# The first sort of a graph kernel carries each edge's weight beside its key, and the record gathers go

## The reference, cut to what matters

```python
x = _layernorm(x + segment_sum(x[src], dst))                        # L0: sum over incoming edges
# L1, ten times, with edge_src = dst and edge_dst = src:
up = jnp.maximum(f[edge_dst] - f[edge_src], 0.0) * sqrt(weights)[:, None]
f  = f + segment_max(up, edge_src)
# L2: three gated graph convolutions; each needs  nw[:, None] * (x @ W)[src]  summed by dst, nw from the edge weights
# L3: a four-layer MLP on (x_i, x_j - x_i) of every edge, averaged by dst
```

## Time and profile before

| what | us |
|---|---|
| three runs | 8461.82, 8480.76, 8480.96 |
| span of the profiled execution | 9642.0 |
| preparation, histogram 0, sort 0, until the first gather | 0 to 589 |
| rest of the sort stage | 589 to 1376 |
| L0 stage, main loop | 1376 to 2549 |
| busy: PE, DVE, ACT, POOL | 6289.8, 6437.2, 3431.3, 3063.5 |
| granted TensorE clock, mean | 0.880 |

### The profile page before, as it was taken

One profiled execution on the slowest core, in us unless ns is written; L12 is line 12 of the kernel. 1 busy time (PEld: TensorE's weight loads), 2 busy tenths in 40 slices (PEclk: granted clock), 3 DMA queues, 4 the chain that ended last, 5 costly groups with the idle time before them and its releaser, 6 DMA issues. The chain is left out here.

```text
span 9642.0 us, 139065 instructions
## 1 busy us (share of the span) xinstructions
PE 6289.8 (65%) x41922; PEld 3109.5 (32%) x41922; DVE 6437.2 (67%) x10345; ACT 3431.3 (36%) x4321; POOL 3063.5 (32%) x2943
## 2 busy tenths in 40 slices
PE   3100120028787979888898879788798989365555
PEld 2100120013443434334343434343344545222222
DVE  8864560017687878787787878787888989433333
ACT  0000000002255545555555555455444444132333
POOL 0047527740032323332232323332300000555553
PEclk9999985559899989999999989899899999677777
DMA  2000001128666667666676666566576767111110
GB/s 83 3 13 1 5 22 25 17 76 294 218 229 202 227 196 238 204 215 218 204 241 200 226 205 235 198 213 213 185 273 232 291 231 290 32 22 22 22 22 24
DMA packets 480504, 1461.81 MB, mean 152 GB/s; under 512 B 109553, under 2 KB 145049, under 8 KB 412582
## 3 DMA queue, kind: packets, MB, share of 16 engines
q1 hardware_dynamic: 228800, 1119.91, 33.6%
q10 hardware_dynamic: 157440, 298.89, 8.7%
q0 software_dynamic: 93568, 33.84, 3.0%
HBM read 1160.35 MB, written 292.22 MB: 151 GB/s over the span
## 5 line engine op out<-in xcount | busy, mean ns | idle before, releaser
L1435 PE MATMUL acc<-dst_hot,parts 128*128 128x512 bf16 x11600 | 3024.8, 387 | 575.1 <-issue 355.7
L1494 ACT ACTIVATE parts_out<-acc 96x1024 bf16<-96x1024 f32 x2320 | 2343.1, 1020 | 2018.0 <-PE acc L1446 1751.2
L1398 POOL DMA_INDIRECT group_best<-best_dram,best_row x1250 | 1361.0, 1089 | 3012.0 <-SPq L1361 2615.7
L1310 DVE TENSOR_SCALAR dst_hot<-dst_rows,node_f 128x2048 bf16<-128x2048 int16 x2910 | 2051.8, 740 | 180.1 <-PE acc L1446 138.7
L1435 PEld LDWEIGHTS acc<-dst_hot,parts 128*128 x11600 | 1057.6, 98 | 1868.2 <-issue 768.6
L914 POOL DMA_INDIRECT gathered<-table_dram,source_index x719 | 731.7, 1018 | 1800.2 <-POOLq L158 1300.5
L309 POOL DMA_INDIRECT got<-edges_dram,record_index x928 | 940.6, 1014 | 860.7 <-DVEq L777 548.8
L1446 PE MATMUL acc<-source,parts 128*128 128x128 bf16 x9280 | 922.6, 223 | 9.8 <-DMA source<-source_dram 4.5
L1446 PEld LDWEIGHTS acc<-source,parts 128*128 x9280 | 640.7, 99 | 642.7 <-issue 361.8
L1517 DVE SCALAR_TENSOR_TENSOR risen<-rise,factor 128x512 f32<-128x512 f32 x580 | 401.1, 692 | 588.0 <-PE rise L1458 322.3
L1523 DVE TENSOR_TENSOR_SCAN best<-joined,best,risen 128x512 f32<-128x512 uint8 x570 | 728.6, 1278 | 0.7
(11 more groups left out here) (376 smaller groups left out, 8013.5 us busy)
## 6 DMA issues: line engine op xcount, KB each, us to landing
dst_rows<-step_dst_dram SPq DMA_DIRECT2D x291, 1024.0 KB, 4.2
source<-source_dram SPq DMA_DIRECT2D x291, 1024.0 KB, 6.7
dst_kept_in<-dst_hot_dram SPq DMA_DIRECT2D x174, 1280.0 KB, 5.6
best_dram<-best_out ACTq DMA_DIRECT2D x580, 256.0 KB
factor<-step_weight_dram ACTq DMA_DIRECT2D x560, 256.0 KB
sources<-source_dram SPq DMA_DIRECT2D x174, 512.0 KB, 6.6
dst_hot_dram<-dst_kept SPq DMA_DIRECT2D x58, 1280.0 KB
src_rows<-step_src_dram SPq DMA_DIRECT2D x58, 512.0 KB
```

The costliest lines, as they stand in the source:

```text
L1310: nc.vector.tensor_scalar(hot[k % 2][b][:, :], index_rows[k // 2 % 2][:, k % 2, :], node_f[:, b:b + 1], None, ALU.is_equal).then_inc(hot_r ...
L1398: pool.indirect_dma_start(group_best[:, g, h, :], None, best_dram, bass.IndirectOffsetOnAxis(ap=best_row[:, i:i + 1], axis=0)).then_inc(en ...
L1435: nc.tensor.matmul(acc[n % 3][:, 0:TILE], blocks[b], hot[k % 2][b][:, q * TILE:(q + 1) * TILE], start=(b == 0), stop=(b == DST_BLOCKS - 1))
L1494: act.activation(moved[n % (2 * QUADS)][:, :], acc[n % 3][0:SPLIT, :], ACT.Copy).then_inc(tile_moved, 1)
```

## The change

The low 17 bits of key 0 now hold the destination's number within its group, plus one (`dst_id`), in place of the edge number. `record`, `edges_dram`, `got`, `record_index`, `group_base` and all 928 gathers go. The weights are loaded into `load[0]`, and each of the 153 stages of sort 0 has three instructions more on VectorE: a comparison of the keys into a mask in PSUM (`out_of_order`), and two predicated copies that exchange the weights (`swap_loads`, called at the head of the next stage, or in `turn` and at the end). Before them ScalarE has copied the whole weight array (`keep_loads`, 128 x 1024). At each turn TensorE transposes the weights as well, and ScalarE copies them. After the sort the weights are stored, loaded back as rows, and turned as the keys are; destinations, weights and roots for L0 and L1 come from these in `slots_by_group`, and are stored in the sort stage. Sort 1 is as before.

```diff
-            for n in range(k * STEP_SUBS, (k + 1) * STEP_SUBS):
-                pool.indirect_dma_start(got[:, n, :], None, edges_dram,
-                                        bass.IndirectOffsetOnAxis(ap=record_index[:, n:n + 1], axis=0)).then_inc(got_in, 16)
...
+                    link(nc.vector.scalar_tensor_tensor(dst_id[0:EP, :], group_key, -float(DST_NODES), dst_in[0:EP, :], ALU.mult, ALU.add))
+                    link(nc.vector.tensor_scalar(dst_id[0:EP, :], dst_id[0:EP, :], 1, None, ALU.add))
...
+            def sort_tensor(pe, turn_ready, turned_done, copied, swapped=None, load_turned=None, load_moved=None):
                 for n in range(turns):
                     pe.wait_ge(turn_ready, n + 1)
                     if n:
                         pe.wait_ge(copied, n)
+                    turn_blocks(turned, ping[0]).then_inc(turned_done, 1)
+                    if swapped:
+                        pe.wait_ge(swapped, STAGES_BEFORE[n])
+                        if n:
+                            pe.wait_ge(load_moved, n)
+                        turn_blocks(load_t, load[STAGES_BEFORE[n] % 2]).then_inc(load_turned, 1)
...
+            def keep_loads(act, s, swapped, kept):
+                if s:
+                    act.wait_ge(swapped, s)
+                act.activation(load[(s + 1) % 2][:, :], load[s % 2][:, :], ACT.Copy).then_inc(kept, 1)
...
+            def sort_scalar_loaded(act, turned_done, copied, loaded, swapped, kept, load_turned, load_moved):
+                act.wait_ge(loaded, 1)
+                for s in range(len(STAGE_BITS)):
+                    if s in STAGES_BEFORE:
+                        n = STAGES_BEFORE.index(s)
+                        act.wait_ge(turned_done, n + 1)
+                        act.activation(ping[0][:, :], turned[:, :], ACT.Copy).then_inc(copied, 1)
+                        act.wait_ge(load_turned, n + 1)
+                        act.activation(load[s % 2][:, :], load_t[:, :], ACT.Copy).then_inc(load_moved, 1)
+                        act.wait_ge(load_moved, n + 1)
+                    keep_loads(act, s, swapped, kept)
...
+                def swap_loads():
+                    s = done[1]
+                    if not swapped or s == done[0]:
+                        return
+                    m = STAGE_BITS[s]
+                    was, to = halves(load[s % 2], m), halves(load[(s + 1) % 2], m)
+                    greater = out_of_order[s % 2].rearrange("p (n w) -> p n w", w=1 << m)
+                    dve.wait_ge(kept, s + 1)
+                    nc.vector.copy_predicated(to[0], greater, was[1])
+                    nc.vector.copy_predicated(to[1], greater, was[0]).then_inc(swapped, 1)
+                    done[1] += 1
 
                 def stage(m):
+                    swap_loads()
+                    a, z = halves(ping[at[0]], m), halves(ping[1 - at[0]], m)
+                    if swapped:
+                        nc.vector.tensor_tensor(out_of_order[done[0] % 2].rearrange("p (n w) -> p n w", w=1 << m), a[0], a[1], ALU.is_gt)
+                    nc.vector.tensor_tensor(z[0], a[0], a[1], ALU.min)
+                    link(nc.vector.tensor_tensor(z[1], a[0], a[1], ALU.max))
                     at[0] = 1 - at[0]
+                    done[0] += 1
...
                     nc.vector.drain().then_inc(turn_ready, 1)
+                    swap_loads()
                     dve.wait_ge(copied, turn_count[0])
...
+                        dve.wait_ge(key_rows_in, 16 * QUADS)
+                        dve.wait_ge(key_rows_turned, 1)
+                        link(V.tensor_scalar(key_rows[:, :, :], key_rows[:, :, :], ID_MASK, None, ALU.bitwise_and))
+                        link(V.tensor_scalar(dst_rows[:, :, :], key_rows[:, :, :], -1, None, ALU.add))
+                        V.drain().then_inc(dst_ready, 1)
                         dve.wait_ge(key_cols_moved, 2)
-                        link(V.tensor_scalar(record_index[:, :], col_key[:, :].bitcast(U32), ID_MASK, None, ALU.bitwise_and))
-                        V.drain().then_inc(edge_ready, 1)
...
+                        link(V.tensor_scalar(col_key[:, :], col_key[:, :], ID_MASK, None, ALU.bitwise_and))
+                        link(V.tensor_scalar(dst_col[:, :], col_key[:, :], -1, None, ALU.add))
+                        dve.wait_ge(load_rows_in, 16 * QUADS)
+                        link(V.tensor_scalar(root_rows[:, :, :], weight_rows[:, :, :], 1e-30, None, ALU.max))
+                        V.drain().then_inc(positive, 1)
+                        dve.wait_ge(load_cols_turned, 1)
+                        link(V.tensor_scalar(weight_rows[:, :, :], weight_rows[:, :, :], 0.0, None, ALU.is_gt))
...
+                        dve.wait_ge(rooted, 1)
+                        link(V.tensor_tensor(root_rows[:, :, :], root_rows[:, :, :], weight_rows[:, :, :], ALU.mult))
+                        V.drain().then_inc(root_rows_ready, 1)
...
+                    link(V.memset(load[0][:, :], 0.0))
+                    link(V.tensor_copy(load[0][0:EP, 0:EF], w_in[0:EP, :]))
+                    V.drain().then_inc(load_ready, 1)
...
-                        if c >= STEPS_FIRST:
-                            dve.wait_ge(got_in[c % 4], records_of(c))
-                            columns_of(slice(c * STEP_SUBS, (c + 1) * STEP_SUBS))
```

More of the change, by code:

```diff
@@ L257, in _ @@
                     nc.vector.memset(keys[0][:, :], float(FILLER << ID_BITS))
[L258 to L263, removed]
+                    link(nc.vector.memset(keys[1][:, :], float((NPAD + KEY_BIAS) << ID_BITS)))
+                    dve.wait_ge(iota_done, 1)
+                    dve.wait_ge(loaded, 32)
                     nc.vector.tensor_scalar(keys[1][:, EF:EF + HI], node_id[:, :], KEY_BIAS, None, ALU.add)
@@ L276, in _ @@
                     link(nc.vector.tensor_scalar(src_id[0:EP, :], src_in[0:EP, :], 1, None, ALU.add))
[L277 to L280, removed]
+                    for o, low_bits in enumerate((dst_id, src_id)):
+                        link(nc.vector.tensor_tensor(keys[o][0:EP, 0:EF], keys[o][0:EP, 0:EF], low_bits[0:EP, :], ALU.bitwise_or))
                     nc.vector.drain().then_inc(keyed, 1)
@@ L349, in program @@
             bit = sb("bit", [P, LOG_N - LOG_F], I32, own)
+            load = [sb(f"load{i}", [P, SORT], F32, own) for i in range(2)]
             turned = own.enter_context(nc.psum_tensor("turned", [P, SORT], F32))
+            load_t = own.enter_context(nc.psum_tensor("load_t", [P, SORT], F32))
             with phase("iota_done", "vec") as (block, iota_done, vec):
@@ L370, in sort_sync, with turn_blocks @@
                              ping[0][:, :].bitcast(I32)).then_inc(keys_out, 16)
-                sp.wait_ge(keys_out, 16)
-            def sort_tensor(pe, turn_ready, turned_done, copied):
+            def turn_blocks(to, of):
+                for b in range(SORT // P):
+                    last = nc.tensor.transpose(to[:, b * P:(b + 1) * P], of[:, b * P:(b + 1) * P], identity[:, :])
+                return last
+            def sort_tensor(pe, turn_ready, turned_done, copied, swapped=None, load_turned=None, load_moved=None):
                 for n in range(turns):
@@ L442, in sort_vector @@
                 nc.vector.drain().then_inc(turn_ready, 1)
+                swap_loads()
             key_rows = sb("key_rows", [STEPS1, QUADS, TILE], I32, own)
+            weight_rows = sb("weight_rows", [STEPS1, QUADS, TILE], F32, own)
+            root_rows = sb("root_rows", [STEPS1, QUADS, TILE], F32, own)
+            dst_rows = sb("dst_rows", [STEPS1, QUADS, TILE], I16, own)
             col_key = sb("col_key", [P, SUBTILES], I32, own)
@@ L559, in _ @@
                     sp.wait_ge(slots_out, 48)
+                    sp.wait_ge(rows_out, 32)
                     sp.wait_ge(zeros_out, 16 * (1 + D // 2))
@@ L1223, in _ @@
                     dve.wait_ge(const_done, 1)
-                    def columns_of(some):
-                        link(V.scalar_tensor_tensor(dst_col[:, some], got[:, some, 0], 1.0, group_base[:, some], ALU.mult, ALU.subtract))
-                    columns_of(slice(0, STEPS_FIRST * STEP_SUBS))
                     for k in range(STEPS1 + 1):
@@ L1265, in _ @@
                     split_rows(link, rows[:, :, :])
-        records.close()
         with ExitStack() as own:
```

171 lines of the change are left out of this document (72 added, 99 removed).

## The result

| | us |
|---|---|
| before, four runs | 8461.82 to 8480.96, median 8475.9 |
| after, four runs | 8562.88 to 8574.01, median 8565.7 |
| after / before | 1.0111, 95% interval 1.0099 to 1.0124 |
| forecast | 8532, range 8385 to 8640 |

A forecast was written before the change was run, and what follows sets the result against it. In plain runs VectorE was taken to bound the sort stage and GpSimd the L0 stage. Terms -225 -4 +280 -17 +13 +4 sum to +51 us on 8481, giving 8532 us, range 8385 to 8640.

The forecast's parts named there:

- a stage of sort 0 that takes over 4 us: Sort 0: the prediction calls itself wrong if a stage takes over 4 us or under 2.7.
- The L0 loop: L0 stage: without its 528 gathers 727 us become 502, -225; bounds -171 (bare gather pace 1.25 us) and -245.
- Three instructions a stage: Sort 0 on VectorE: comparison and two predicated copies, 0.61 us each over 153 stages, +280; bounds +203 and +445.
- the turns: Sort 0's fourteen turns: one swap each falls into VectorE's wait, -17 us; weights late afterwards, +13 us.
- Rival D: Sort 0: predicated copies are dear, two passes of about 1.15 us, +165, total time 8697 us; chance 0.10.
- A: Whole kernel: as forecast, slower by 51 us, predicated copies at 0.57 to 0.68 us, total 8500 to 8570; chance 0.50.
- E: Sort 0: predicated copies are cheap, 0.36 us each, -77, total time 8455 us; chance 0.11.
- The 400 gathers of the sort stage: Sort stage: removing them gives nothing, as VectorE's chain ends later anyway; bounds 0 to -60 (pace of 1.5 us).
- a port rule: Gathers beside VectorE: two-port instructions keep GpSimd from writing descriptors; as a rival, total time 8385 us, chance 0.10.
- Between the sorts: Slots work between the sorts: SyncE's store and four loads +1.6 us, uncovered product of the roots +2.4, together +4.
- The account of the stall: Profile before: 659 of 1161 us excess is a profiling backlog beside gathers, absent from plain runs; 502 in later layers.
- Rival B: Sort and L0 stages: the stall is partly the chip's own, 66 to 217 us more saved, 8466 to 8315; chance 0.18.

The follow-up runs named there:

- before_none: The kernel before without any of its 928 record gathers, GpSimd writing zeros in their place: 8238.9 us, ratio 0.9709.
- before_no_late: The kernel before without the last 528 record gathers, those of the L0 stage, GpSimd writing zeros in their place: 8300.5 us, ratio 0.9776.
- before_again: The kernel before with no edit, profiled a second time: span 8481.7 us, ratio 0.9985 to runs of the same kernel.

## Why the prediction was right, and where it wasn't

It was right in kind: a sort that VectorE paces pays for three more instructions in each of 153 stages, and a loop paced by GpSimd gets its gathers back. By one of its own signs of being wrong, a stage of sort 0 that takes over 4 us, it failed in part: 46 stages have dear copies, and where nothing hides them the next minima start 4.24 us later or more. By terms:

- *The L0 loop, forecast -229 with the turn of `dst_col`, measured -194.* The step without gathers was 8.22 us ((1955.7-1487.0)/57 in the row below), forecast 8.39. The loop before took 687 us, not 727: the pace of 1.35 came out of the disturbed profile; in the second it is 1.282. The bound I had at the bare pace, -171, was the better guess.

```profile
L1276 DVE TENSOR_SCALAR source_made<-src_rows,node_f x58: 744/748/755, 1487.0 to 1955.7; 128x2048 bf16<-128x2048 int16 x58
```

- *Three instructions a stage, forecast +280, and -4 for the turns; measured +316.* The step "I take 0.61" held for 107 of 153 stages. In the 46 with runs of one or two columns, two copies take 1.10 each, 0.98 more together. Fourteen of these stand before a turn; their copies ran in VectorE's wait for ScalarE there, and a turn grew by 0.6 us only, as forecast. In the other 32 they count, and with a comparison that comes 0.1 us later behind them make some 36 us. VectorE's waits after turns were 21.9 us in all for 14, where I had 0.95 each, 13 us: 9 more. The cheap stages came out 5 us shorter than forecast (3.11 to 3.15 us where I had 3.16). Rival D's price of 1.15 was right for the 46, A's 0.61 for the others, E's 0.36 for none; no rival had a cost that depends on the run.
- *The 400 gathers of the sort stage, forecast 0, measured -37 in the windows and -40 by `before_none`.* This step failed in substance: "nothing, since VectorE's chain ends later anyway". The account let GpSimd end at 1129 at 1.35 us a gather; it ended at 1193 at 1.50. The bound of -60 for just this pace was mis-sized as well: it left out the 20 us by which VectorE was to end later, and would have been -40, which is what came. The evidence against a port rule was a gather beside the one-hots of the earlier trace rows, 0.32 us each and so too short to hold a gather for long:

```profile
8586.36 5.04 DVE L2102 TENSOR_SCALAR hot<-index_rows,node_f 128x512 bf16<-128x512 int16 x16 [0.30 <-DVE message L2111]
```

  Histogram 1's instruction is 2.83 us long. In the disturbed trace two of its forty steps ran beside the 400, while the sort stage was stalled, and they showed it already; I hadn't read them:

```profile
1095.49 2.86 DVE L675 TENSOR_TENSOR one_low<-low,ramp 125x2560 bf16<-125x2560 bf16 x1 [2.43 <-remote]
...
1096.75 2.42 POOL L309 DMA_INDIRECT got<-edges_dram,record_index  x1 [0.30 <-issue]
...
1103.28 2.83 DVE L675 TENSOR_TENSOR one_low<-low,ramp 125x2560 bf16<-125x2560 bf16 x1 [2.19 <-issue]
1103.47 3.46 POOL L309 DMA_INDIRECT got<-edges_dram,record_index  x1 [0.30 <-issue]
```

- *Between the sorts, forecast +4, measured +10*: the issue of four loads on SyncE, 8.05 us where the earlier trace rows had 1.30. VectorE's wait grew by 7.9 us, and the product of the roots took 2.3.
- *Preparation, forecast 0 within 3, measured -6.*

The errors make the 32 us between +51 and +83: loop +35, sort 0 +40, between the sorts +6, sort stage -37, sort 1 -2, preparation -6, behind -4. Two of 35 to 40 went one way and one the other, so the forecast's closeness is partly luck; without the missed 37 us it would have been 69 us off.

The account of the stall was half right: plain runs have none, and sort 1's end at 896 was right (its last minimum is at 896.8). The L0 loop's end, 1163+727 = 1890 against a measured 1888, came out by luck: the stage started 38 us later than that and the loop took 40 us less. The cause it gave isn't borne out: profiling kernels with these gathers doesn't bring the stall as such, since four further profiles of kernels with 400 or 928 of them have none. What disturbed that execution stays open. Rival B falls with the 190 us of `before_no_late`.

## What to carry to other kernels

When a profiled execution is 14% longer than the runs, take another profile before splitting the excess. Where GpSimd issues gathers beside VectorE, look at each of VectorE's long instructions by name, with one tensor input or two: each held back the gather that started inside it until 0.81 us after its own end, and cutting it in linked parts lets more gathers through, for about 0.17 us a part here (0.32 for two, 0.70 for four). Test such a rule on a long instruction, not on short ones. Price a predicated copy by its runs: with runs of one or two 4-byte columns it cost nearly twice what a minimum over the same columns does.

## What the runs showed of the hardware

A predicated copy of 512 columns (f32, int32 mask) takes 0.61 us in a row of instructions, and 1.10 where destination and data come in runs of one or two columns; the minima over the same strides stay at 0.60. With the mask in SBUF or PSUM it is the same. 1024 contiguous columns take 1.19. Gathers of 8-byte records are issued 1.25 us apart with VectorE free, 1.33 beside the sort's pairs of minimum and maximum (the pace of the pairs), 1.88 beside histogram 1, and 1.28 beside the L0 stage's one-hots. A gather that starts more than 0.1 us into a VectorE instruction ends 0.81 us after that one's end, or after its own 0.94 us if that is later (464 of 480 such gathers of `before_again`, to within 0.03 us); so it was for a comparison with two tensor inputs and for a one-hot with one. A linked part of a cut instruction cost 0.85 us for 0.71 of work. The mean granted clock was 0.88 or 0.93 for the same kernel (after: 0.932 in two runs and 0.875 in two) with run times that don't follow it: 8566.1 and 8574.0 at 0.932, 8565.3 and 8562.9 at 0.875.
